# Gated cross-attention and a routed feed-forward: the causal mask and the row maxima put into one tile by GpSimd

## The chip, the cores and the metric

One core of one Trainium2 chip. The engines are TensorE (PE, with its weight loads PEld), VectorE (DVE), ScalarE (ACT), GpSimd (POOL) and SyncE (SP), whose queue issues most DMAs. The metric is the device time of one execution in microseconds, as the median of several executions.

## The reference

Only what matters is shown. There are 32 sequences of 128 tokens with 256 features, 16 heads of 16, 8 experts of 1024, and each token goes to its 2 best experts.

```python
q, k, v = proj(layernorm(x), w_q, b_q), proj(ctx, w_k, b_k), proj(ctx, w_v, b_v)
scores = einsum('bhqd,bhkd->bhqk', q, k) / sqrt(16)
attn = softmax(where(j <= i, scores, -inf))          # causal: S = 128
x = x + tanh(g_xattn) * (einsum('bhqk,bhkd->bhqd', attn, v) @ w_o.T + b_o)
xf = layernorm(x)
logits = xf @ Wr + br                                 # 8 experts
weights = softmax(where(logits >= second_best, logits, -inf))
h = gelu(einsum('td,edh->eth', xf, W1) + b1)
x = x + tanh(g_ffn) * einsum('etd,te->td', einsum('eth,ehd->etd', h, W2) + b2, weights)
```

## The kernel before, in words

The program has two halves. The first (`attention_and_routing`) does the attention of all 32 sequences, finds each token's experts and scatters the token rows to regions of experts in HBM (`xs_dram`). The second (`experts`) goes through 39 tiles of 256 rows, applies two layers, and adds the results to the output rows by indirect DMA. The change lies in the first half.

**Groups and slots.** The first half takes 16 groups of 2 sequences (`GT = 2`, blocks b = 0 and 1). One pass of `it(g, ...)` of each engine has 8 slots (`QUADS`), n = 0 to 7. A slot deals with one quad, that is 4 heads of one block: 128x512 scores. Passes are pipelined: in the pass of group g the quads of g are done, the projections of g + 1 are made, the output projection, second normalisation and logits of g - 1, and the routing table and scatters of g - 2. The order on each engine is the order in which the slots are written down; engines meet at counting semaphores only.

**A quad's way.** In slot n PE writes the scores of quad n with the queries on partitions into PSUM bank `SB[n % 2]` (L899; the constant rows of `qfull` and `kfull` make later keys very negative, so that the maximum is over the keys seen). DVE takes the maxima over keys (L746, `rowmax`, 128x4 in 16 bits). In slot n + 1 PE makes the transposed scores less their maximum in bank `TB` ("ST" below) in three steps, all accumulated in one bank: the causal mask by a product of `ident16` with `maskT`, 512 columns wide (L955); the negative maxima by four products of `rowmax`, broadcast, with `negident` (L958); the scores by four products of 96 rows (L962). ACT takes the exponential (L583, `probs`). In slot n + 3 PE multiplies by the values, with a column of ones for the sums (L979, "PV" below). After four quads of a block DVE divides (`normalise`, L695 and L696, result `ao`), in slot 7 for block 0 of group g and in slot 3 for block 1 of group g - 1.

**What else stands in the slots, as far as it is spoken of below.**
- PE: transposes of `cin` and the product with `wo` (slot 0), the key product and transposes of `xn` (1), values (2), the query product (3), the product with `wo` of block 1 (4), logits (7). The first product with `wo` waits for `logits_read` and `w_read`, which DVE gives in slot 7.
- ACT: `cT` after the exponential of slot 0, `keys` in slot 1, `queries` in slot 3, and parts of the expert weights' split in slots 1 to 6.
- DVE: slot 0 `xn` (L763), `x2` of block 0 (L706), then the scale of the expert weights (`ebits`, `wnow`, L771 to L778, with copies to `wscale` and `wsquares`); slot 1 `k_rest` (L675), the normalised rows `pay` of block 0 (L715, `norm2`), the routing table; slot 2 its end (`sel`, L808), third part of keys (L687); slot 3 `va`, `q_rest`; slot 4 `x2` of block 1 (L706) and its variance; slot 5 `pay` of block 1 (L715) and the third part of queries (L687); slots 2, 3, 6 and 7, behind the maxima, the low half of the weights (L756, both inputs in SBUF); slot 7 the statistics of the next input, the weights' sum `wsum` (L845), the logits `lg` (L848), the top two, and the masks `msk` (f32) and `msk16`.
- POOL: slots 1 and 5 the power -1/2 of a variance (L497), which `norm2` of the same slot waits for; slot 5 the input with the output bias added (`xb`, L504, 128x512 with two inputs); slots 4 to 7 one scatter each (L512); slot 7 the power for `xn` (L521).

DVE's wait for the buffer of `rowmax` is for the ST two quads before:

```python
dve.wait_ge(s_psum, g * QUADS + n + 1)
when(dve, n >= 2 or there(g - 1), st_psum, g * QUADS + n - 1)
dve.tensor_reduce(rowmax[n % 2][:, :], SB[n % 2][:, :]..., AX, ALU.max).then_inc(max_ready, 1)
```

Of the kernel before, what the change touches and what calls it, by code (L numbers as in the profile page):

```python
# [12 lines left out]
P = 128  # L13
# [18 lines left out]
MASKED = -1e30  # L32
# [62 lines left out]
def bass_flamingo(nc, x, ctx_in, g_xattn, g_ffn, w_q, b_q, w_k, b_k, w_v, b_v, w_o, b_o,  # L95
# [4 lines left out]
    with ExitStack() as stack:  # L100
        def sb(name, shape, dt=F32):
            return stack.enter_context(nc.sbuf_tensor(name, shape, dt))
# [25 lines left out]
        ident16 = sb("ident16", [P, P], BF16)  # L128
        qsteps, ksteps, maskT = (sb(name, [P, P], BF16) for name in ("qsteps", "ksteps", "maskT"))
# [44 lines left out]
def attention_and_routing(nc, env):  # L174
# [3 lines left out]
     xs_dram, w_dram, bank, qst, kst, qfull, kfull, ident, negident, ident16, qsteps, ksteps, maskT, earlier, ones16, rank1,  # L178
# [4 lines left out]
         "negident", "ident16", "qsteps", "ksteps", "maskT", "earlier", "ones16", "rank1", "rank0", "ones8", "region0",  # L183
         "base", "mostsel", "tgx", "tgf", "gates_in", "power", "wscale", "wsquares", "padrow",
         "b1t", "stage", "split", "all_slots", "wts", "tile_no_int", "numbers_made", "weights_in"))
    with ExitStack() as stack:
# [21 lines left out]
        rowmax = [sb(f"rowmax{i}", [P, 4], BF16) for i in range(2)]  # L208
        probs = [sb(f"probs{i}", [P, 4, P]) for i in range(4)]
# [14 lines left out]
        msk, msk16 = sb("msk", [P, GT, E]), sb("msk16", [P, GT, E], BF16)  # L224
# [31 lines left out]
        s_psum, max_ready = sem("s_psum"), sem("max_ready")  # L256
# [81 lines left out]
        with nc.Block() as block:  # L338
# [107 lines left out]
            def _(pool):  # L446
# [4 lines left out]
                step.later(pool.memset(maskT[:, :], 0.0))  # L451
# [40 lines left out]
                def it(g, par, half, stays, stayed):  # L492
                    for n in range(QUADS):
                        if n in (1, 5) and there(g - 1):
# [4 lines left out]
                        if n == 5 and there(g + 1):  # L499
# [53 lines left out]
            def _(act):  # L553
# [12 lines left out]
                def it(g, par, half, stays, stayed):  # L566
                    g1, p1 = g + 1, 1 - par
                    for n in range(QUADS):
# [8 lines left out]
                        q, pg = (QUADS - 1, g - 1) if n == 0 else (n - 1, g)  # L577
# [67 lines left out]
            def _(dve):  # L645
# [6 lines left out]
                dve.wait_ge(consts, 9)  # L652
# [4 lines left out]
                step.later(dve.tensor_scalar(negident[:, :], ident[:, :], -1.0, None, ALU.mult))  # L657
                dve.tensor_copy(ident16[:, :], ident[:, :]).then_inc(dve_consts, 1)
# [756 lines left out]
```

## Time and profile before

| | us |
|---|---|
| median of 3 runs | 938.75 (936.92 to 939.47) |
| the profiled execution | 942.84 |
| its span, first to last instruction | 940.9 |
| scores and maxima of the 16 groups (L746) | 34.8 to 444.9 |
| PE busy in the span | 846.5 |
| DVE busy | 600.4 |
| ACT busy | 442.3 |
| POOL busy | 257.6 |

In rows of the profile, PE is the matmuls and PEld the weight loads beside them. The number after the time is the length; what stands in square brackets is the engine's idle time before the instruction and what ended it. In the groups by line, "x128" is the count, and the number behind the busy time is the mean length in ns.

### The profile page before, as it was taken

Reading aid. Unit: us, or ns where it says so; the run is one execution under the profiler, and the core shown is the slowest. Engines: PE = TensorE matmul, PEld = TensorE weight load, DVE = VectorE, ACT = ScalarE, POOL = GpSimd, SP = SyncE. Lnnn points to the kernel's source line nnn. Section 1 sums busy time; section 2 is a strip of 40 time slices with the busy share of each in tenths; the row PEclk is TensorE's granted clock in tenths of the full one; section 3 lists DMA queues with packets and bytes.
Section 4 is the critical chain, followed back from the end, with each engine's and each line's share of the span. In section 5 each row is a group of like instructions: output and inputs, shape, how many; then the busy total and the mean of one; then the engine's idle time right before and its main releaser. Section 6 shows DMA issues by size and latency. Waiting matters only on the chain. (4 is left out here: it accounts for less than half of the span.)

```text
span 940.9 us, 24425 instructions
## 1 busy us (share of the span) xinstructions
PE 846.5 (90%) x7600; PEld 750.5 (80%) x7601; DVE 600.4 (64%) x1521; ACT 442.3 (47%) x962; POOL 257.6 (27%) x239
## 2 busy tenths in 40 slices
PE   3599999999999999999539999999999999999990
PEld 2488888888888888888338789998989998989980
DVE  2357888888888888887636555555555555555540
ACT  2155555655555555654224444554444455544440
POOL 3001333222332333323210322232332232223332
PEclk9699999999999999999659999999999999999996
DMA  8765666665667787864388432323233233322222
GB/s 185 141 135 132 158 152 129 139 155 156 155 159 202 188 185 176 174 164 156 130 288 295 87 53 48 54 53 53 48 50 52 48 59 50 51 48 36 30 24 25
DMA packets 87944, 108.77 MB, mean 116 GB/s; under 512 B 12832, under 2 KB 81568, under 8 KB 85664
## 3 DMA queue, kind: packets, MB, share of 16 engines
q1 hardware_dynamic: 72448, 87.17, 37.4%
q0 software_dynamic: 14304, 19.15, 12.7%
q8 instruction: 60, 0.98, 0.5%
q10 hardware_dynamic: 1088, 1.11, 0.4%
q14 instruction: 44, 0.36, 0.1%
HBM read 46.82 MB, written 34.36 MB: 86 GB/s over the span
## 5 line engine op out<-in xcount | busy, mean ns | idle before, releaser
L1220 POOL DMA_INDIRECT out_rows<-yg,xs x78 | 126.6, 1624 | 332.7 <-ACT yg L1262 190.3
L1352 PE MATMUL bank<-xh,wts 128*128 128x256 f16 x1872 | 214.2, 275 | 0.0
L1368 PE MATMUL bank<-wts,hh 128*128 x1872 | 210.6, 273 | 0.0
L1352 PEld LDWEIGHTS bank<-xh,wts 128*128 x1872 | 185.0, 99 | 22.5
L1368 PEld LDWEIGHTS bank<-wts,hh 128*128 128x128 f16 x1872 | 183.2, 98 | 21.2
L1252 ACT ACTIVATE hf<-bank,b1t,gscale 128x256 f32<-128x256 f32 x312 | 154.7, 562 | 24.3 <-PE bank L1352 24.3
L979 PE MATMUL bank<-va,probs 128*128 128x102 f32 x1024 | 139.7, 278 | 8.1 <-DVE ao L696 8.1
L979 PEld LDWEIGHTS bank<-va,probs 128*128 128x128 f32 x1024 | 124.2, 192 | 10.7 <-DVE ao L696 6.2
L1262 ACT ACTIVATE yg<-yb,xs 128x256 f32<-128x256 f32 x78 | 35.4, 500 | 199.5 <-DVE yb L1301 199.5
L583 ACT ACTIVATE probs<-bank 128x512 f32<-128x512 f32 x128 | 76.9, 601 | 101.8 <-PE bank L962 95.2
L1291 DVE SCALAR_TENSOR_TENSOR hh<-hf,hscale,hh 128x512 f16<-128x512 f32 x156 | 117.1, 751 | 5.6
L512 POOL DMA_INDIRECT token_rows<-pay,slots x64 | 76.2, 1190 | 130.4 <-DVE slots L811 93.0
L746 DVE TENSOR_REDUCE rowmax<-bank 128x4 bf16<-128x512 f32 x128 | 87.7, 686 | 22.8 <-PE bank L899 12.8
L1301 DVE SCALAR_TENSOR_TENSOR yb<-bank,yscale,b_all 128x512 f32<-128x512 f32 x39 | 29.2, 750 | 108.7 <-PE bank L1368 108.7
L1290 DVE TENSOR_SCALAR hh<-hf,hscale 128x512 f16<-128x512 f32 x156 | 76.1, 488 | 20.9 <-ACT hf L1252 12.3
L1275 DVE SCALAR_TENSOR_TENSOR xh<-bank,xh 128x512 f16<-128x512 f32 x39 | 27.0, 691 | 70.3 <-ACT xh L1243 70.3
L899 PE MATMUL bank<-wts 128*128 128x128 bf16 x512 | 49.9, 220 | 17.2 <-DMA wts<-queries 15.8
L497 POOL TENSOR_TENSOR rs<-mv,power 128x1 f32<-128x1 f32 x32 | 17.7, 552 | 153.3 <-DVE mv L665 153.3
L899 PEld LDWEIGHTS bank<-wts 128*128 128x128 bf16 x512 | 40.2, 102 | 20.5 <-issue 17.6
L955 PE MATMUL bank<-maskT,ident 128*128 128x512 bf16 x128 | 49.1, 383 | 6.4 <-issue 3.1
L958 PEld LDWEIGHTS bank<-negident,rowmax 128*128 128x128 bf16 x512 | 39.5, 98 | 19.1 <-issue 0.6
L962 PE MATMUL bank<-wts 96*128 96x128 bf16 x512 | 49.7, 219 | 0.0
(169 smaller groups left out, 1082.0 us busy)
## 6 DMA issues: line engine op xcount, KB each, us to landing
wts<-in_W SPq DMA_DIRECT2D x16, 1024.0 KB, 7.9
wts<-keys SPq DMA_DIRECT2D x96, 128.0 KB
wts<-queries SPq DMA_DIRECT2D x96, 128.0 KB
xs<-token_rows SPq DMA_DIRECT2D x39, 272.0 KB
split_weights<-wts SPq DMA_DIRECT2D x8, 1024.0 KB, 4.6
wts<-split_weights SPq DMA_DIRECT2D x8, 1024.0 KB
xin<-in_x SPq DMA_DIRECT2D x16, 256.0 KB, 4.0
cin<-in_ctx_in SPq DMA_DIRECT2D x16, 256.0 KB, 4.2
```

The costliest lines, as they stand in the source:

```text
L512: pool.indirect_dma_start(out=xs_dram[:, :], out_offset=bass.IndirectOffsetOnAxis(ap=slots[par][:, b, r:r + 1], axis=0), in_=pay[par][:, b ...
L583: act.activation(probs[q % 4][:, :, :].rearrange("p a q -> p (a q)"), TB[q % 2][:, :], ACT.Exp, scale=float(DK) ** -0.5).then_inc(exp_read ...
L746: dve.tensor_reduce(rowmax[n % 2][:, :], SB[n % 2][:, :].rearrange("p (a k) -> p a k", a=4), AX, ALU.max).then_inc(max_ready, 1)
L899: last = pe.matmul(ps[:, a * P:(a + 1) * P], qfull[par][:, h, tok], kfull[par][:, h, tok], start=True, stop=True)
L962: last = pe.matmul(ps[:, a * P:(a + 1) * P], kst[i][:, h, tok], qst[i][:, h, tok], start=False, stop=a == 3)
L979: last = pe.matmul(OB[:, h * VA:(h + WIDE) * VA], probs[m % 4][:, a, :], va[i][:, b, h, :].unsqueeze(1).to_broadcast([P, WIDE, VA]), start ...
L1220: pool.indirect_dma_start(out=out[:, :], out_offset=bass.IndirectOffsetOnAxis(ap=numbers, axis=0), in_=yg[m % 2][:, half, :], in_offset=No ...
L1252: last = act.activation(hf[:, c, :], HB[quarter][:, c % 2 * TILE:(c % 2 + 1) * TILE], ACT.Gelu, bias=b1t[:, bass.ds(e, 1), c], scale=gscal ...
L1290: step(dve.tensor_scalar(high, full, hscale[:, bass.ds(e, 1)], None, ALU.mult))
L1291: dve.scalar_tensor_tensor(out=hh[b][:, 1, c, :].rearrange("p c t -> p (c t)"), in0=full, scalar=hscale[:, bass.ds(e, 1)], in1=high, op0=A ...
L1352: last = pe.matmul(HB[c // 2][:, c % 2 * TILE:(c % 2 + 1) * TILE], wts[:, bass.ds(expert[1], 1), at:at + P], xh[b][:, xp, k, :], start=q = ...
L1368: last = pe.matmul(YB[b][:, half * D:(half + 1) * D], hh[b][:, hp, c, half * P:(half + 1) * P], wts[:, bass.ds(expert[0], 1), at:at + D], ...
```

## The change

GpSimd makes a tile `cover` (128x512, 16 bits, two buffers in the memory of `first_xs[0]`, which is not otherwise used before the second half). An `affine_select` reads `rowmax`, broadcast over 128 columns, and puts +1e30 where the key lies after the query. PE's ST becomes, for each head, a product of `cover` with `negident` and the scores' product; the product with `maskT` and the tiles `maskT` and `ident16` go. ST and the exponential lag the maxima by two slots in place of one; PV stays at three. DVE's maxima wait for `cover_ready` and not for ST, and the cover waits for the maxima and for the ST two quads before. Besides:
- `xb` moves from slot 5 to slot 6, the scatters from slots 4 to 7 to slots 3, 4, 5 and 7. In slots 1 and 5 the cover stands ahead of the power.
- The f32 `msk` goes, and the routing reads `msk16`.
- DVE no longer copies `wnow` to `wscale` for each weight; four small operations in `tile_table` make the scales from `wsquares`, and the copy to `wsquares` is no longer waited for at once.
- One GpSimd memset, one `affine_select` and one DVE copy go from the constants.

```diff
-MASKED = -1e30
+MASKED = 1e30
...
+        cover = [env["first_xs"][0][:, :, :].rearrange("p h r -> p (h r)")[:, 256 * i:256 * i + 256].bitcast(BF16)
+                 .rearrange("p (a k) -> p a k", a=4) for i in range(2)]
...
-                pool.affine_select(out=maskT[:, :], in_=maskT[:, :], compare_op=ALU.is_ge,
-                                   fill=MASKED, base=0, pattern=[[1, P]],
-                                   channel_multiplier=-1).then_inc(consts, 1)
...
                     for n in range(QUADS):
+                        if there(g):
+
+                            pool.wait_ge(max_ready, g * QUADS + n + 1)
+                            settled(pool)
+                            when(pool, n >= 2 or there(g - 1), st_psum, g * QUADS + n - 1)
+                            settled(pool)
+                            pool.affine_select(out=cover[n % 2][:, :, :],
+                                               in_=rowmax[n % 2][:, :].unsqueeze(2).to_broadcast([P, 4, P]),
+                                               compare_op=ALU.is_ge, fill=MASKED, base=0, pattern=[[0, 4], [-1, P]],
+                                               channel_multiplier=1).then_inc(cover_ready, 1)
                         if n in (1, 5) and there(g - 1):
...
-                        if n == 5 and there(g + 1):
+                        if n == 6 and there(g + 1):
...
-                        if n >= 4 and there(g - 2):
-                            b, r = (n - 4) // 2, n % 2
-                            if n == 4:
+                        if n in (3, 4, 5, 7) and there(g - 2):
+                            b, r = divmod((3, 4, 5, 7).index(n), 2)
+                            if n == 3:
...
-                        q, pg = (QUADS - 1, g - 1) if n == 0 else (n - 1, g)
+                        q, pg = (QUADS + n - 2, g - 1) if n < 2 else (n - 2, g)
...
-                            when(dve, n >= 2 or there(g - 1), st_psum, g * QUADS + n - 1)
+                            when(dve, n >= 2 or there(g - 1), cover_ready, g * QUADS + n - 1)
...
-                            dve.wait_ge(w_scaled, g)
                             e = half - (1 - par)
-                            dve.tensor_copy(wscale[:, p1, bass.ds(e, 1)], wnow[:, p1:p1 + 1])
-                            step(dve.tensor_copy(wsquares[:, p1, bass.ds(e, 1)], wsum[:, p1:p1 + 1]))
+                            step.later(dve.tensor_copy(wsquares[:, p1, bass.ds(e, 1)], wsum[:, p1:p1 + 1]))
...
-                            step.later(dve.tensor_tensor(msk[:, :, :], lg[:, :, :],
-                                                         mx[:, :, 1:2].to_broadcast([P, GT, E]), ALU.is_ge))
...
-                        if there(g if n >= 1 else g - 1):
-
-                            tg, m, i = (g, n - 1, par) if n >= 1 else (g - 1, QUADS - 1, p1)
+                        if there(g if n >= 2 else g - 1):
+
+                            tg, m, i = (g, n - 2, par) if n >= 2 else (g - 1, QUADS + n - 2, p1)
                             tok = slice((m // 4) * P, (m // 4) * P + P)
-                            pe.wait_ge(max_ready, tg * QUADS + m + 1)
+                            pe.wait_ge(cover_ready, tg * QUADS + m + 1)
                             when(pe, m >= 2 or there(tg - 1), exp_ready, tg * QUADS + m - 1)
                             ps = TB[m % 2]
-                            pe.matmul(ps[:, :], ident16[:, :], maskT[:, :].unsqueeze(1).to_broadcast([P, 4, P]),
-                                      start=True, stop=False)
-                            for a in range(4):
-                                pe.matmul(ps[:, a * P:(a + 1) * P], rowmax[m % 2][:, a:a + 1].to_broadcast([P, P]),
-                                          negident[:, :], start=False, stop=False)
                             for a in range(4):
                                 h = 4 * (m % 4) + a
+                                pe.matmul(ps[:, a * P:(a + 1) * P], cover[m % 2][:, a, :],
+                                          negident[:, :], start=True, stop=False)
                                 last = pe.matmul(ps[:, a * P:(a + 1) * P], kst[i][:, h, tok],
-                                                 qst[i][:, h, tok], start=False, stop=a == 3)
+                                                 qst[i][:, h, tok], start=False, stop=True)
...
+    for layer in range(2):
+        step(dve.tensor_scalar(smallint[:, 2, :], wsquares[:, layer, :].bitcast(I32), 24, None, ALU.logical_shift_right))
+        step(dve.tensor_scalar(wscale[:, layer, :].bitcast(I32), smallint[:, 2, :], -one, 204 * one, ALU.mult, ALU.add))
```

## Rows read from the trace of the kernel before

**Rows 1.** The page's busy time of each engine: us, share of span, instructions

```profile
PE 846.5 (90%) x7600; PEld 750.5 (80%) x7601; DVE 600.4 (64%) x1521; ACT 442.3 (47%) x962; POOL 257.6 (27%) x239
```

**Rows 2.** Busy time in one stretch: us, each engine's busy (x instructions), clock, DMA

```profile
200.00:250.00 50.00, 48.14 (x439) 42.41 (x438) 41.87 (x123) 26.86 (x63) 15.58 (x16) 1.00 0.63 152
```

**Rows 3.** The first and the last of 14 such rows of L706, DVE's timeline: start, us

```profile
76.27 0.48 DVE L706 SCALAR_TENSOR_TENSOR x<-bank,tgx,xb 128x256 f32<-128x256 f32 x1 [1.01 <-PE bank L880]
...
418.32 0.48 DVE L706 SCALAR_TENSOR_TENSOR x<-bank,tgx,xb 128x256 f32<-128x256 f32 x1 [1.01 <-PE bank L880]
```

**Rows 4.** DVE's timeline through one group: start, us, instruction, idle before it

```profile
196.61 0.87 DVE L675 SCALAR_TENSOR_TENSOR k_rest<-bank,bqk,keys 128x256 f32<-128x256 f32 x2 [0.60 <-ACT keys L562]
...
205.69 0.88 DVE L675 SCALAR_TENSOR_TENSOR q_rest<-bank,bqk,queries 128x256 f32<-128x256 f32 x2 [0.49 <-ACT queries L562]
...
208.09 0.48 DVE L706 SCALAR_TENSOR_TENSOR x<-bank,tgx,xb 128x256 f32<-128x256 f32 x1 [0.93 <-PE bank L880]
...
209.46 0.69 DVE L746 TENSOR_REDUCE rowmax<-bank 128x4 bf16<-128x512 f32 x1
...
210.13 1.36 DVE L715 TENSOR_SCALAR pay<-x,mv,rs 128x256 f32<-128x256 f32 x1
...
211.42 0.68 DVE L687 TENSOR_TENSOR queries<-q_rest,queries 128x512 bf16<-128x512 f32 x1
...
212.62 0.73 DVE L756 SCALAR_TENSOR_TENSOR wts<-wts,wnow 128x512 f32 x1
...
213.56 0.42 DVE L696 TENSOR_TENSOR ao<-bank,rden 128x256 f32<-128x256 f32 x1
...
214.49 0.74 DVE L756 SCALAR_TENSOR_TENSOR wts<-wts,wnow 128x512 f32 x1
...
216.52 0.16 DVE L848 TENSOR_TENSOR lg<-bank,br_all 128x16 f32<-128x16 f32 x1
...
222.70 0.88 DVE L675 SCALAR_TENSOR_TENSOR k_rest<-bank,bqk,keys 128x256 f32<-128x256 f32 x2 [0.70 <-ACT keys L562]
...
223.49 0.40 DVE L715 TENSOR_SCALAR pay<-x,mv,rs 128x256 f32<-128x256 f32 x1
```

**Rows 5.** TensorE's timeline in the same group: start, us, instruction, idle before it

```profile
216.93 1.03 PE L880 MATMUL bank<-wo_sb,aoT 128*128 128x256 f32 x4
...
222.19 0.38 PE L955 MATMUL bank<-maskT,ident 128*128 128x512 bf16 x1
...
222.41 0.38 PE L958 MATMUL bank<-negident,rowmax 128*128 128x128 bf16 x4
...
222.63 0.39 PE L962 MATMUL bank<-wts 96*128 96x128 bf16 x4
```

**Rows 6.** GpSimd's timeline in the same group

```profile
209.54 0.56 POOL L497 TENSOR_TENSOR rs<-mv,power 128x1 f32<-128x1 f32 x1 [5.78 <-DVE mv L665]
...
210.08 1.26 POOL L504 TENSOR_TENSOR xb<-xin,bo_all 128x512 f32<-128x512 f32 x1
...
211.52 1.49 POOL L512 DMA_INDIRECT token_rows<-pay,slots  x1 [0.18 <-issue]
...
213.31 0.97 POOL L512 DMA_INDIRECT token_rows<-pay,slots  x1 [0.30 <-issue]
```

**Rows 7.** The timeline at the start of the kernel

```profile
22.54 1.26 POOL L504 TENSOR_TENSOR xb<-xin,bo_all 128x512 f32<-128x512 f32 x1 [14.35 <-DVE bo_all L729]
...
22.82 1.52 DVE L687 TENSOR_TENSOR queries<-q_rest,queries 128x512 bf16<-128x512 f32 x1 [0.43 <-ACT queries L601]
```

**Rows 8.** The groups by line that price what is removed or added: busy, mean

```profile
L460 POOL TENSOR_SCALAR_AFFINE_SELECT ident<-ident 128x128 f32<-128x128 f32 x1 | 0.3, 299 | 0.0
...
L469 POOL IOTA ints<- 128x8 int32 x1 | 0.1, 139 | 0.0
```

**Rows 9.** The timeline where the two halves meet

```profile
474.64 0.17 DVE L1100 TENSOR_TENSOR yscale<-small 128x8 f32<-128x8 f32 x1
...
480.29 0.40 SPq L441 DMA_DIRECT2D xs<-token_rows  x1
```

More of the change, by code:

```diff
@@ L127, in bass_flamingo @@
         negident = sb("negident", [P, P], BF16)
-        ident16 = sb("ident16", [P, P], BF16)
-        qsteps, ksteps, maskT = (sb(name, [P, P], BF16) for name in ("qsteps", "ksteps", "maskT"))
+        qsteps, ksteps = (sb(name, [P, P], BF16) for name in ("qsteps", "ksteps"))
         earlier = sb("earlier", [P, P], BF16)
@@ L177, in attention_and_routing @@
     (x, ctx_in, g_xattn, g_ffn, w_q, b_q, w_k, b_k, w_v, b_v, w_o, b_o, W1, b1, W2, Wr, br, out,
-     xs_dram, w_dram, bank, qst, kst, qfull, kfull, ident, negident, ident16, qsteps, ksteps, maskT, earlier, ones16, rank1,
+     xs_dram, w_dram, bank, qst, kst, qfull, kfull, ident, negident, qsteps, ksteps, earlier, ones16, rank1,
      rank0, ones8, region0, base, mostsel, tgx, tgf, gates_in, power, wscale, wsquares, padrow,
@@ L223, in attention_and_routing @@
         lg, mx, lgs = sb("lg", [P, GT, E]), sb("mx", [P, GT, 8]), sb("lgs", [P, GT, E])
-        msk, msk16 = sb("msk", [P, GT, E]), sb("msk16", [P, GT, E], BF16)
+        msk16 = sb("msk16", [P, GT, E], BF16)
         ex, em, esum, erec = sb("ex", [P, GT, E]), sb("em", [P, GT, E]), sb("esum", [P, GT]), sb("erec", [P, GT])
@@ L255, in attention_and_routing @@
         v_psum, va_ready = sem("v_psum"), sem("va_ready")
-        s_psum, max_ready = sem("s_psum"), sem("max_ready")
+        s_psum, max_ready, cover_ready = sem("s_psum"), sem("max_ready"), sem("cover_ready")
         st_psum, exp_ready = sem("st_psum"), sem("exp_ready")
@@ L450, in _ @@
                 step.later(pool.memset(ksteps[:, :], -FUTURE / STEP))
-                step.later(pool.memset(maskT[:, :], 0.0))
                 step.later(pool.memset(earlier[:, :], 1.0))
@@ L651, in _ @@
                 step.later(dve.memset(ones16[:, :], 1.0))
-                dve.wait_ge(consts, 9)
+                dve.wait_ge(consts, 8)
                 step.later(dve.tensor_copy(rank0[:, :], ints[:, 0, :]))
@@ L656, in _ @@
                 step.later(dve.tensor_copy(base[:, :], ints[:, 2, :]))
-                step.later(dve.tensor_scalar(negident[:, :], ident[:, :], -1.0, None, ALU.mult))
-                dve.tensor_copy(ident16[:, :], ident[:, :]).then_inc(dve_consts, 1)
+                dve.tensor_scalar(negident[:, :], ident[:, :], -1.0, None, ALU.mult).then_inc(dve_consts, 1)
                 step.wait()
@@ L785, in it @@
                             dve.wait_ge(ex_ready, g - 1)
-                            step(dve.tensor_tensor(em[:, :, :], ex[:, :, :], msk[:, :, :], ALU.mult))
+                            step(dve.tensor_tensor(em[:, :, :], ex[:, :, :], msk16[:, :, :], ALU.mult))
                             for b in range(GT):
-                                step.later(dve.tensor_tensor_scan(cnt[:, b, :], ones8[:, :], msk[:, b, :], 0.0,
+                                step.later(dve.tensor_tensor_scan(cnt[:, b, :], ones8[:, :], msk16[:, b, :], 0.0,
                                                                   ALU.mult, ALU.add))
@@ L791, in it @@
                             step.later(dve.reciprocal(erec[:, :], esum[:, :]))
-                            step.later(dve.tensor_tensor(cm[:, :, :], cnt[:, :, :], msk[:, :, :], ALU.mult))
+                            step.later(dve.tensor_tensor(cm[:, :, :], cnt[:, :, :], msk16[:, :, :], ALU.mult))
                             step(dve.tensor_tensor(mostsel[:, :], mostsel[:, :], cnt[:, :, E - 1], ALU.max))
```

2 lines of the change are left out of this document (1 added, 1 removed).

## The prediction

> **What bounds the kernel now.** I read the page's busy times first, then the first half's busy time by stretches, then the timelines of DVE, PE and POOL through one group, and last who waited for whom. The page makes PE look like the bound, at 90% [rows 1]; in the stretch from 200 to 250 us, all of it first half, PE is busy 96% and DVE 84% of the time, at full granted clock [rows 2]. But the profile draws each matmul longer than the distance to the next, so a short gap of PE's does not show. The timelines show more: the pace is set by a loop that passes from one engine to the other. A group repeats every (418.32 - 76.27) / 13 = 26.31 us [rows 3]. I cut it at three places [rows 4].
> 1. From L706 (`x2`, second block) at 208.09 to the end of `ao` at 213.98: 5.89 us, all DVE without a pause. L706 itself had waited 0.93 us for PE.
> 2. From `ao` to `k_rest` (L675) at 222.70: 8.72 us. `ao` releases PE; PE's product with `wo` at 216.93 [rows 5] also needs `wsum` and `lg` (end 216.68), so DVE's slot 7 and PE's slot 7 end together, with 0.15 us over semaphore time of 0.10 to spare. Then ST, exp, `cT`, the key product and `keys` follow, and DVE waits 0.70 us.
> 3. From `k_rest` to the next L706, 196.61 to 208.09: 11.48 us, limited by PE; DVE waited 0.49 us at `q_rest` and 0.93 us at L706, so its own work is 10.06 us.
>
> **What is removed.** The mask product costs PE the distance from its start to L958's, 222.41 - 222.19 = 0.22 us [rows 5], times 128 = 28 us at most; it counts only in segments that PE limits. Segment 2 contains one ST (-0.22), segment 3 four (11.48 - 0.88 = 10.60). In segment 1 none counts. On DVE, the f32 `msk` and the copy of `wscale` with its waits go, about 0.4 us a group, after `lg` and before `k_rest`; DVE waits at `k_rest` anyway, so neither is worth anything. The two constants less at the start and the second PE lag at the end I cost at nothing: the first hides behind the loads, and the last PV keeps its slot. The four small DVE operations added at the table's end, each about 0.2 us like L1100 with its wait, end near 475.7 us, well ahead of the first load of `xs` at 480.29 [rows 9]; without that cover they would cost 0.8 us once.
>
> **What a cover costs.** No row shows a mask of 128x512. Half of the two-input sum of that size (L504, 1.26 us [rows 6]) is 0.63 us; a line through the 8 columns of L469 (139 ns) and the 128 of L460 (299 ns) gives 0.81 us at 512; four times L460 gives 1.20 us [rows 8]. I take 0.75 us, between the first two, since an instruction has a fixed part that four separate ones would pay four times, and keep 0.63 and 1.20. Eight of them add 6 us to POOL's 15.6 us in 50 [rows 2]: its throughput suffices; what matters is what stands behind each.
>
> **The powers queue behind the cover.** In slots 1 and 5 POOL now makes cover(n) before L497. Before, L497 at 209.54 ran while DVE did the maxima of slot 5, so that L715 followed at 210.13 [rows 4, 6]. Now cover(5) can start only after those maxima (210.15), and L715 needs: 0.10 for the semaphore, 0.75 cover, 0.56 power, 0.10 semaphore, so it starts at 211.66. Its 1.36 us shrinks to 0.41, the length of an undisturbed one (0.40 at 223.49), because the bias sum no longer runs beside it. The old start of the next, L687, was 211.42; the new is 211.66 + 0.33 = 211.99. Segment 1: +0.57. In slot 1, cover(1) must also wait for the ST of that slot, whose last product ends at 222.63 + 0.39 = 223.02 [rows 5], so at 222.80 without the mask product; 0.10 + 0.75 + 0.56 + 0.10 puts L715 at 224.35 in place of 223.49: +0.86 in DVE's part of segment 3.
>
> **The bias sum meets another instruction.** L715 beside L504 took 1.36 us for 0.40 [rows 4, 6], and L687, begun 0.28 us into an L504, 1.52 us for 0.68 [rows 4, 7]: DVE's instructions with both inputs in SBUF, and its `tensor_scalar` from SBUF to SBUF, stand still while POOL works on SBUF. The reverse shows too: the L512 at 211.52, just behind the start of an L687, took 1.49 us for the 0.97 of the next [rows 6]. So moving L504 to slot 6 frees L715, but cover(6) waits for L756 of slot 6 (212.62 + 0.74 = 213.36, now 213.93), ends at 214.72, and L504 begins about 214.77; L756 of slot 7, which came at 214.49 and now wants 215.06, is 0.29 us into it and loses the 0.84 us that L687 lost. That is upstream of `lg`, where PE has 0.15 us to spare: +0.69. Segment 2: +0.69 - 0.22 = +0.47. The Trainium skill (SBUF — State Buffer, Who interferes with whom) says that a DVE instruction with two SBUF inputs and a GpSimd one that reads SBUF exclude each other for the whole instruction; the two pairs of rows agree, and by that rule each cover is such an instruction. The GPSIMD Engine Reference of the Trainium skill (3.1) gives 769 ns for 512 elements of a simple GpSimd loop, which would make each cover 0.02 us dearer than I take it.
>
> **The covers meet others.** A cover's semaphore arrives about 0.1 us after the maxima end, when DVE's L756 has already begun (slots 2, 3, 6, 7), so the cover waits, not DVE. Behind it stand `va`, `q_rest`, `normalise` and `bn_stats`, which read PSUM or one operand: nothing. Only in slot 2 does another such operation follow, L808, which may lose nothing, if it is let in ahead of the waiting cover, or some 0.6 us; no row decides; I take 0.30. Segment 3 by DVE: 10.06 + 0.86 + 0.30 = 11.22; by PE 10.60; so 11.22 - 11.48 = -0.26.
>
> **The other moves.** Scatters now stand in slots 3, 4, 5 and 7, each behind a cover. They wait for nothing new and nobody in the first half waits for them before two groups on; a cover behind one waits at most its 1.5 us, and with two slots between cover and ST, 3.3 us each on average (26.31 / 8), ST does not see it. The extra slot also lets PE pass the maxima of slots 5 and 6, but these waits end at `ao` anyway. SP's queue has no new wait.
>
> **The sum.** 0.57 + 0.47 - 0.26 = +0.78 us a group, times 13 = +10.1 us. The first and the last group, where PE gains about 0.2 us in some slots and POOL falls behind in others, I take at zero. The profiled execution took 942.84 us for a span of 940.9; it would become 952.9. It stands 4.1 us above the median of the runs, so against those the forecast is 938.75 + 10.1 = 949 us. Bounds: a cover of 0.63 and nothing at L808 give 0.78 - 0.24 - 0.30 = +0.24, or 942; a cover of 1.20 and 0.60 at L808 give 0.78 + 0.90 + 0.30 = +1.98, or 964. So 942 to 964 is the forecast's own range.
>
> **Rivals.**
> - *PE sets the pace* (faster). If DVE's waits on POOL fall into time that it has over, each group loses the eight mask products, 1.76 us, 13 x 1.76 = 23 us, with the ends up to 28: 913 to 916 us. For it: 96% busy [rows 2]. Against it: DVE's unbroken 5.89 us in segment 1. It decides if the cover and power of slot 5 together take no more than the 0.95 us that L715 lost before. Chance 0.17.
> - *No collisions, only the powers.* If L504 misses L756 and L808 loses nothing: 0.57 - 0.22 - 0.55 = -0.20 a group, -2.6 us, 936 us. Here 0.55 is 11.48 less DVE's 10.06 + 0.86 with a cover of 0.75. For it: a shift of L504 by 1 us is enough. Against: DVE and POOL both start from the same maxima, so their distance is fixed. With a cover of 0.63, 0.12 goes off twice: -0.44 a group, 933 us. Where the power of slot 1 finds DVE waiting besides, segment 3 falls to PE's 10.60 and the sum to -0.65, 930 us. Chance 0.25, of which 0.14 stay within 0.3%.
> - *POOL late in slot 7.* Cover(6), L504, cover(7), L512 and L521 now stand in a row before `xn` of slot 0. L504 ends at 216.03, then come L756 of slot 7 (0.74), the cover (0.75), the scatter with its 0.30 of issue (1.27) and L521, which is like L497 with two columns (0.7 by estimate): 219.5. New `lg` ends at 216.68 + 0.57 + 0.84 = 218.09, and `xn` comes behind it and the maxima of slot 0, not before 219.5 either. A dearer cover tips it, by up to 0.5 us a group: 13 x 0.5 = 6.5 more, 955 us. Chance 0.10.
> - *The product is not really saved*: if the interleaved cover and score products pay for the mask product, ST keeps its 0.66 us: the 0.22 of segment 2 comes back, +1.0 a group, 952 us. Against it: PE issues four of either in 0.22 us now (222.41 to 222.63 [rows 5]), a weight load with each. Chance 0.03.
>
> **Numbers.** The forecast has 0.45; a measurement of this kernel tells about 0.3% (2.8 us) from no change. Slower: 0.45 less 0.02 near 941, plus 0.10 and 0.03 for the two rivals above it = 0.56. Same: 0.14 and 0.02 = 0.16. Faster: 0.17 and 0.11 = 0.28. The range of 8 in 10 leaves out the fastest 0.17 and a little at the top: 926 to 963.
>
> **What would show it.** In the new trace: no L955; ST 0.44 us long; covers of 0.75 us, longer where L756 came first; L715 of slot 5 0.41 us long but 1.5 us after the maxima, released by L497; L756 of slot 7 near 1.6 us; the group's period 27.1 us. I am wrong if L504 and L756 of slot 7 do not overlap, or if DVE's idle time before L715 is short, or if PE still runs without gaps and the period falls below 26.

## The result and the profile after

The changed kernel takes 979.00 us (972.58 to 986.14, four runs) against 939.04 us (936.92 to 939.47) for the kernel before on the same chip: a ratio of 1.043 (1.036 to 1.051). The forecast was 949 us with a range of 926 to 963. The sign was right, and the loss is four times as large as forecast, 40 us for 10. The profiled execution took 972.58 us for a span of 970.8 us, so it stands 6.4 us below the median. Its granted clock has a mean of 0.945; the three longer executions, of 978.24, 979.76 and 986.14 us, have 0.937, 0.933 and 0.928.

The page of the changed kernel, its busy times and the granted clock by fortieths of the span:

```profile
PE 841.9 (87%) x7472; PEld 757.5 (78%) x7473; DVE 595.8 (61%) x1492; ACT 439.1 (45%) x962; POOL 346.3 (36%) x365
PEclk9799899899999999998857999999999999999996
```

PE does less work than before (128 instructions fewer) in a longer span. The clock line has slices of 8 at the fifth and the eighth place, and from the nineteenth on (437 us) it sinks further, as it did from the twentieth in the kernel before. In the kernel before, the clock stood at full from 60 to 456 us. Now it falls to half, 1.2 GHz, four times in groups 2 to 5 (from 110.4, 141.1 and 171.8 us for 6.8 us each, before them from 83.1 us for 3.4 us), and again from 448.3 us, ahead of the last scores. The expectations below call such a fall an episode.

DVE's timeline through one undisturbed group of the changed kernel, to be laid beside [rows 4]; L680 is `k_rest`, L720 `pay`, L811 `sel`, L701 `ao`, L711 `x2`, L692 the third part of queries, L761 the low half of the weights, L851 `lg`:

```profile
319.45 0.88 DVE L680 SCALAR_TENSOR_TENSOR k_rest<-bank,bqk,keys 128x256 f32<-128x256 f32 x2 [1.22 <-ACT keys L568]
...
320.99 0.41 DVE L720 TENSOR_SCALAR pay<-x,mv,rs 128x256 f32<-128x256 f32 x1 [0.66 <-POOL rs L503]
...
324.49 0.72 DVE L811 TENSOR_TENSOR sel<-sel,pos 128x128 f32<-128x128 f32 x1
...
326.94 0.42 DVE L701 TENSOR_TENSOR ao<-bank,rden 128x256 f32<-128x256 f32 x1
...
331.32 0.48 DVE L711 SCALAR_TENSOR_TENSOR x<-bank,tgx,xb 128x256 f32<-128x256 f32 x1 [0.71 <-PE bank L881]
...
332.68 0.69 DVE L751 TENSOR_REDUCE rowmax<-bank 128x4 bf16<-128x512 f32 x1
334.90 0.41 DVE L720 TENSOR_SCALAR pay<-x,mv,rs 128x256 f32<-128x256 f32 x1 [1.53 <-POOL rs L503]
335.23 0.68 DVE L692 TENSOR_TENSOR queries<-q_rest,queries 128x512 bf16<-128x512 f32 x1
...
337.38 0.42 DVE L701 TENSOR_TENSOR ao<-bank,rden 128x256 f32<-128x256 f32 x1
337.72 0.68 DVE L751 TENSOR_REDUCE rowmax<-bank 128x4 bf16<-128x512 f32 x1
338.32 1.14 DVE L761 SCALAR_TENSOR_TENSOR wts<-wts,wnow 128x512 f16<-128x512 f32 x1
...
346.65 0.88 DVE L680 SCALAR_TENSOR_TENSOR k_rest<-bank,bqk,keys 128x256 f32<-128x256 f32 x2 [1.01 <-ACT keys L568]
```

GpSimd's timeline in the same group (the cover is shown as `xs`, whose memory it uses):

```profile
320.31 0.54 POOL L503 TENSOR_TENSOR rs<-mv,power 128x1 f32<-128x1 f32 x1
324.24 0.83 POOL L496 TENSOR_SCALAR_AFFINE_SELECT xs<-rowmax 128x512 bf16<-128x512 bf16 x1 [3.39 <-DVE rowmax L751]
...
333.71 0.62 POOL L496 TENSOR_SCALAR_AFFINE_SELECT xs<-rowmax 128x512 bf16<-128x512 bf16 x1 [0.99 <-PE bank L960]
334.31 0.56 POOL L503 TENSOR_TENSOR rs<-mv,power 128x1 f32<-128x1 f32 x1
...
336.85 0.82 POOL L496 TENSOR_SCALAR_AFFINE_SELECT xs<-rowmax 128x512 bf16<-128x512 bf16 x1 [0.62 <-DVE rowmax L751]
337.65 1.26 POOL L510 TENSOR_TENSOR xb<-xin,bo_all 128x512 f32<-128x512 f32 x1
```

And PE's timeline, where it now waits three times:

```profile
327.42 1.14 PE L977 MATMUL bank<-va,probs 128*128 128x102 f32 x8 [0.97 <-DVE ao L701]
...
335.37 0.44 PE L875 MATMUL bank<-ident,pay 128*128 128x128 f32 x2 [0.87 <-DVE pay L720]
...
337.86 1.14 PE L977 MATMUL bank<-va,probs 128*128 128x102 f32 x8 [1.36 <-DVE ao L701]
```

The prediction's three segments, at full clock, come out of these rows as follows (before, forecast, after). Segment 1, L711 at 331.32 to the end of `ao` at 337.80: 5.89, 6.46, **6.48**. Segment 2, to `k_rest` at 346.65: 8.72, 9.19, **8.85**. Segment 3, 319.45 to 331.32: 11.48, 11.22, **11.87**. The period of this group is thus 27.20 us, where the three forecasts add up to 26.87. The forecast of 27.1 was for the mean of the groups; the eight periods at full clock, of groups 6 to 13, have a mean of 27.28.

In the groups whose clock fell, segment 2 is longer: 10.56 to 12.11 us in groups 2 to 5. PE's timeline of one of them, through the same two waits:

```profile
138.16 0.44 PE L875 MATMUL bank<-ident,pay 128*128 128x128 f32 x2 [0.87 <-DVE pay L720]
...
140.65 1.63 PE L977 MATMUL bank<-va,probs 128*128 128x102 f32 x8 [1.36 <-DVE ao L701]
...
145.72 1.91 PE L881 MATMUL bank<-wo_sb,aoT 128*128 128x256 f32 x4
```

The product with `wo` takes 1.91 us where [rows 5] has 1.03. Busy time by stretches shows the same; the columns are those of [rows 2], the clock behind the engines:

```profile
134.00:141.00 7.00, 4.77 (x58) 4.41 (x57) 5.21 (x12) 4.49 (x12) 5.02 (x7) 1.00 0.59 134
141.00:148.00 7.00, 7.00 (x37) 6.45 (x37) 4.58 (x17) 0.38 (x1) 3.47 (x4) 0.51 0.72 213
```

PE was busy 4.77 of 7 us ahead of the fall, and is then busy without a pause at half speed.

**Where the 30 us between the two profiles went.** The last maxima end 30.8 us later than before (they start at 475.64 in place of 444.85), and what follows takes 0.9 us less. From the starts of slot 0's maxima: the 12 periods from group 2 to group 14 have a mean of 28.25 us for 26.31, which is 23.2 us; the first two give back 0.95; the last period and the last group cost 3.3 and 5.4. Of the 23.2, some 13 us is the longer period at full clock (12 x 1.1, with the mean period of 27.42 us that experiment 5 has without falls), and some 10 us the clock.

### The profile page after: what moved, and what is told of

It reads as the page before. It is cut to its first block and busy times, and to the rows that moved or that the text cites. A ratio compares the mean times of both kernels' runs of the same rounds, so it can differ in the third digit from the quotient of the medians.

```text
span 970.8 us, 24729 instructions
## 1 busy us (share of the span) xinstructions
PE 841.9 (87%) x7472; PEld 757.5 (78%) x7473; DVE 595.8 (61%) x1492; ACT 439.1 (45%) x962; POOL 346.3 (36%) x365
## 5 line engine op out<-in xcount | busy, mean ns | idle before, releaser
L496 POOL TENSOR_SCALAR_AFFINE_SELECT xs<-rowmax 128x512 bf16<-128x512 bf16 x128 | 97.4, 762 | 240.4 <-DVE rowmax L751 140.4
L977 PE MATMUL bank<-va,probs 128*128 128x102 f32 x1024 | 143.5, 283 | 37.4 <-DVE ao L701 35.3
L977 PEld LDWEIGHTS bank<-va,probs 128*128 128x128 f32 x1024 | 127.5, 196 | 42.4 <-DVE ao L701 27.6
L958 PE MATMUL bank<-negident,xs 128*128 128x128 bf16 x512 | 75.0, 223 | 0.3 <-POOL xs L496 0.3
L518 POOL DMA_INDIRECT token_rows<-pay,slots x64 | 67.2, 1050 | 22.1 <-issue 11.6
L960 PE MATMUL bank<-wts 96*128 96x128 bf16 x512 | 75.0, 223 | 0.0
L900 PEld LDWEIGHTS bank<-wts 128*128 128x128 bf16 x512 | 41.6, 105 | 19.0 <-issue 16.1
L960 PEld LDWEIGHTS bank<-wts 96*128 96x128 bf16 x512 | 51.4, 100 | 4.8 <-issue 1.9
```

The lines of the kernel that those rows point to most:

```text
L496: pool.affine_select(out=cover[n % 2][:, :, :], in_=rowmax[n % 2][:, :].unsqueeze(2).to_broadcast([P, 4, P]), compare_op=ALU.is_ge, fill=M ...
L900: last = pe.matmul(ps[:, a * P:(a + 1) * P], qfull[par][:, h, tok], kfull[par][:, h, tok], start=True, stop=True)
L960: last = pe.matmul(ps[:, a * P:(a + 1) * P], kst[i][:, h, tok], qst[i][:, h, tok], start=False, stop=True)
L977: last = pe.matmul(OB[:, h * VA:(h + WIDE) * VA], probs[m % 4][:, a, :], va[i][:, b, h, :].unsqueeze(1).to_broadcast([P, WIDE, VA]), start ...
```

## The experiments

All times are medians; ratios are to the kernel before, with the 95% interval.

**1. The powers ahead of the cover** (`pow_first`, from the changed kernel).

```diff
                     for n in range(QUADS):
+                        if n in (1, 5) and there(g - 1):
+                            b = n // 4
+                            pool.wait_ge(var2_ready, (g - 1) * GT + b + 1)
+                            pool.tensor_tensor(rs2[:, b:b + 1], mv2[:, b, 1:2], power[:, 0:1],
+                                               ALU.pow).then_inc(rstd2_ready, 1)
                         if there(g):
...
-                        if n in (1, 5) and there(g - 1):
...
```

> The changed kernel with only this edit: in slots 1 and 5 GpSimd makes the power before the cover, not behind it. Theory A (GpSimd's queue order costs 1.0 us a group, and the idle time it makes on PE lets PE's clock fall): the stretch from L706 to ao falls from 6.49 us to 5.1 to 5.5, the group's period at full clock from 27.3 to 26.0 or less, the half-clock episodes of groups 2 to 5 get fewer, and the time is 935 to 955 us. Rival B (the clock falls because the mask product is gone, whatever the waits): the stretch shortens the same, but the episodes stay, and the time is 958 to 968 us.

950.31 us, 1.014 (1.007 to 1.020): one exchange of two blocks gives back 29 of the 40 us. Part of this is the clock, which fell less: its profile has 17 us at half clock between 60 and 430 us (falls from 160.8, 188.1, 369.0 and 423.6 us), where the changed kernel's has 24. Segment 1 falls to 4.94 us, below the 5.89 of before, since `pay` neither waits nor meets `xb`; segment 3 falls to 11.11. But `xb` now collides in full in slot 7. The timeline of this kernel, GpSimd, DVE and then PE:

```profile
211.92 0.65 POOL L501 TENSOR_SCALAR_AFFINE_SELECT xs<-rowmax 128x512 bf16<-128x512 bf16 x1
212.12 2.23 DVE L761 SCALAR_TENSOR_TENSOR wts<-wts,wnow 128x512 f32 x1
212.52 1.27 POOL L510 TENSOR_TENSOR xb<-xin,bo_all 128x512 f32<-128x512 f32 x1
...
215.89 1.10 PE L881 MATMUL bank<-wo_sb,aoT 128*128 128x256 f32 x4 [1.17 <-DVE lg L851]
```

DVE's 0.74 us instruction starts inside a cover and is held until `xb`, next in GpSimd's queue, is over too: 1.49 us lost at once, `lg` late, PE waiting 1.17 us. Segment 2 is 9.93 us. That is the collision the prediction feared for the changed kernel, in another one, and it costs more than the 0.84 us of the forecast.

**2. One more product ahead of each ST** (`filler`, from the changed kernel): 512 columns of constants into the bank that ST then overwrites.

```diff
                             ps = TB[m % 2]
+                            pe.matmul(ps[:, :], negident[:, :], earlier[:, :].unsqueeze(1).to_broadcast([P, 4, P]),
+                                      start=True, stop=True)
```

> The changed kernel plus a product of 512 columns ahead of each ST, whose result is overwritten at once: PE does more work than in the changed kernel, and the output is the same. Theory A (some 20 of the 40 us are PE's half-clock episodes, and these come from PE having less to do): the granted clock is back at 0.955 or more, no episode lies in groups 2 to 14, and the time is 950 to 962 us although work was added. Rival C (all of the loss is waits): the product adds up to 0.2 us in each of 5 STs on the path, and the time is 979 to 992 us.

984.01 us, 1.049 (1.043 to 1.055), as rival C had it and not as theory A. The clock still fell, from 110, 168, 195, 257 and 311 us. Work put where PE does not wait does not fill the waits (PE still waits 1.14 us for `ao` in slot 7); it adds to the path (segment 3 went to 12.3 us).

**3. The mask product taken out of the kernel before** (`no_mask`). Nothing takes its place, so this kernel leaves out the causal mask. As in the change, the products of the maxima and of the scores now alternate head by head.

```diff
-                            pe.matmul(ps[:, :], ident16[:, :], maskT[:, :].unsqueeze(1).to_broadcast([P, 4, P]),
-                                      start=True, stop=False)
...
+                                pe.matmul(ps[:, a * P:(a + 1) * P], rowmax[m % 2][:, a:a + 1].to_broadcast([P, P]),
+                                          negident[:, :], start=True, stop=False)
```

> The kernel before without the mask product, all else as before (the exponentials include the keys after the query). Theory A with its PE part: segments 2 and 3 lose 0.2 and 0.9 us, the period falls from 26.3 to 25.3, and the time is 922 to 928 us if the clock holds. Rival B (losing the product alone makes PE's clock fall): half-clock episodes appear in groups 2 to 14 and the time is 940 to 965 us.

928.83 us, 0.989 (0.983 to 0.995). The segments are 5.89, 8.52 and 10.68 us, the period 25.28 for 26.31: the product is worth 1.03 us a group, against 0.22 + 0.88 = 1.10 by the prediction's step. Segment 1 has none of it. With the rest of the kernel as it was, the product is thus worth 10 us, not the 23 of the first rival. And the clock stays at full from 59.4 to 421.2 us, so the product's absence alone did not make it fall.

**4. Covers that nobody reads, in the kernel before** (`dead_cover`): the changed kernel's GpSimd block ahead of the powers; ST as before. DVE's maxima wait for it besides.

```diff
                     for n in range(QUADS):
+                        if there(g):
+                            pool.wait_ge(max_ready, g * QUADS + n + 1)
...
+                            when(pool, n >= 2 or there(g - 1), st_psum, g * QUADS + n - 1)
...
+                            pool.affine_select(out=cover[n % 2][:, :, :], ...).then_inc(cover_ready, 1)
...
                             when(dve, n >= 2 or there(g - 1), st_psum, g * QUADS + n - 1)
+                            when(dve, n >= 2 or there(g - 1), cover_ready, g * QUADS + n - 1)
```

> The kernel before, where GpSimd also makes the covers ahead of the powers as in the changed kernel, but nobody reads them; PE's work and its lag of one slot are as before, xb stays in slot 5. Theory A: the stretch from L706 to ao grows by 0.5 to 1.3 us (powers behind the cover, and xb now meets L687 or L756), the period is 27.0 to 27.8, and the time is 950 to 960 us if PE's clock holds at 0.95 or more. Rival D (PE's idle time makes the clock fall even with the mask product kept): episodes appear, and the time is 965 to 985 us.

995.63 us, 1.058 (1.050 to 1.065), above the ranges of both theories. Segment 1 is 7.46 us, since `pay` waits for the power and still meets `xb` there (1.35 us long), and the clock falls seven times between 107 and 419 us, though PE has all its work of before. PE's timeline in this kernel:

```profile
224.44 0.44 PE L887 MATMUL bank<-ident,pay 128*128 128x128 f32 x2 [1.13 <-DVE pay L727]
```

So it is not the mask product's absence that lets the clock fall: falls come with the product in place, and in experiment 3 they stayed away without it. They go with the waits.

**5. Work only in the two waits** (`idle_filler`, from the changed kernel): four products of constants in slot 6 ahead of the wait for `pay`, five in slot 7 ahead of the wait for `ao`, each 512 columns.

```diff
+                            if n == 7:
+                                free_bt(pe, g, 5)
+                                for _ in range(5):
+                                    pe.matmul(BT[:, :], negident[:, :], earlier[:, :]..., start=True, stop=True)
                             if m % 4 == 0:
                                 when(pe, b == 1 or there(tg - 1), ao_ready, tg * GT + b)
...
-                            pe.wait_ge(xn2_ready, (g - 1) * GT + b + 1)
                             free_bt(pe, g, 2 if n == 2 else 4)
+                            if n == 6:
+                                for _ in range(4):
+                                    pe.matmul(BT[:, :], negident[:, :], earlier[:, :]..., start=True, stop=True)
+                            pe.wait_ge(xn2_ready, (g - 1) * GT + b + 1)
```

> The changed kernel plus nine products of 512 columns a group whose result nobody reads, put where PE stands idle: four ahead of its wait for pay in slot 6, five ahead of its wait for ao in slot 7. The output is the same. Theory E (PE's clock falls because of these idle stretches, of 1.1 and 1.4 us): no half-clock episode in groups 2 to 14, segments 6.5, 8.9 and 11.9 us, period 27.3, time 952 to 958 us. Rival F (the episodes do not come from PE's idle time): they stay, and the time is 975 to 990 us.

960.74 us (960.17 to 961.88), 1.022 (1.020 to 1.025): 18 us faster than the changed kernel (20 by the two ratios) by giving PE 144 useless products. Its PE timeline:

```profile
295.19 1.02 PE L997 MATMUL bank<-earlier,negident 128*128 128x512 bf16 x4
296.46 0.44 PE L875 MATMUL bank<-ident,pay 128*128 128x128 f32 x2 [0.24 <-DVE pay L720]
...
297.46 1.24 PE L973 MATMUL bank<-earlier,negident 128*128 128x512 bf16 x5
298.95 1.14 PE L982 MATMUL bank<-va,probs 128*128 128x102 f32 x8 [0.24 <-DVE ao L701]
```

The waits shrink from 0.87 and 1.36 us to 0.24 each, nothing on DVE's path changes (6.49, 8.84, 11.87, period 27.42), and the clock stays at full from 39.8 to 446 us. PE's third wait, for `ao` in slot 3, was not filled: it stays, with 0.67 to 1.58 us in the 13 groups from 2 to 14, and no fall came behind it. The spread of the runs falls from 13.6 us to 1.7. Busy time from 50 to 450 us, first of the kernel before, then of the changed one, then of this one, each from its own profile:

```profile
50.00:450.00 400.00, 381.85 (x3505) 338.17 (x3503) 326.33 (x999) 218.40 (x496) 111.60 (x114) 1.00 0.67 162
```

```profile
50.00:450.00 400.00, 350.26 (x3149) 319.61 (x3148) 302.93 (x906) 203.13 (x467) 184.34 (x224) 0.96 0.63 151
```

```profile
50.00:450.00 400.00, 375.26 (x3377) 326.81 (x3374) 310.25 (x940) 208.06 (x477) 189.09 (x229) 0.99 0.64 157
```

**6. The small edits alone** (`small_edits`, from the kernel before): `xb` in slot 6, scatters in slots 3, 4, 5 and 7, `msk16` only, no copy to `wscale`; powers, mask product and lag as before.

```diff
-                        if n == 5 and there(g + 1):
+                        if n == 6 and there(g + 1):
...
-                        if n >= 4 and there(g - 2):
-                            b, r = (n - 4) // 2, n % 2
+                        if n in (3, 4, 5, 7) and there(g - 2):
+                            b, r = divmod((3, 4, 5, 7).index(n), 2)
...
```

> The kernel before with the side edits alone: xb in slot 6, scatters in slots 3, 4, 5 and 7, msk16 only, fewer copies of scales; mask product and lag as before. Theory G: the collision only moves from L715 of slot 5 to an L756, so the period stays within 0.3 us of 26.3, and the time is 934 to 944 us. Rival H: xb in slot 6 finds DVE free of two-operand work, the stretch from L706 to ao falls to 4.95 us, and the time is 925 to 930 us.

948.95 us, 1.010 (1.007 to 1.013), slower, against my expectation. Segments 5.86, 8.72, 11.48 are those of before. The profile shows why nothing is won: `pay` is down to 0.41 us, and in its place the low half of the weights in slot 6 takes 1.66 us for 0.74. The collision has moved within segment 1. It now stands just ahead of `ao`, PE waits 0.93 us there in place of 0.44, and the clock fell twice, from 215.9 and 349.0 us. The profiled run is only 2.5 us above that of before; what makes the median 8 us worse was not seen in a trace. The granted clock of the three longer executions, 0.949 to 0.954 for the profiled one's 0.958, points to more such falls in them.

**7 to 10. Where `xb` can stand.** It was moved from the pass before into the pass of its own group (it is read only one pass later): to slot 3, with SP's input loads put behind the copies of keys so that the earlier release fits, from the kernel before (`xb_own`) and, with the powers first and the scatters in slots 3, 5, 6 and 7, from the changed one (`pow_xb_own`); and to slot 0, with SP's order unchanged, from either (`before_xb0`, `pow_xb0`).

```diff
-                        if n == 5 and there(g + 1):
-                            arrived(pool, x_loaded, g + 1, 1 - par)
-                            when(pool, there(g - 1), x2_ready, g * GT)
+                        if n == 0 and there(g):
+                            arrived(pool, x_loaded, g, par)
+                            when(pool, there(g - 2), x2_ready, (g - 1) * GT)
...
-                            pool.tensor_tensor(xb[1 - par][:, :, :], xin[1 - par][:, :, :],
+                            pool.tensor_tensor(xb[par][:, :, :], xin[par][:, :, :],
...
```

The edit shown is that of `before_xb0`.

> The kernel before with xb made in the group's own pass in slot 3, where DVE reads PSUM for 3 us (and SyncE's loads of the next inputs put behind the copies of the keys, since they wait for xb). Theory G: L715 takes 0.41 us in every slot, the stretch from L706 to ao falls from 5.89 to 4.94 us, the other segments stay, and the time is 925 to 929 us. Rival I: PE or the loads then limit, and the time is 934 to 942 us.

931.80 us, 0.991 (0.988 to 0.994), between the ranges of the two theories: segment 1 is 5.06 us. What `xb` cost before is thus some 0.83 us a group.

> The changed kernel with the powers ahead of the covers, xb made in the own pass in slot 3, and scatters in slots 3, 5, 6 and 7. By the three segments: 4.94, 8.5 to 8.9 (L756 of slot 7 no longer blocked by xb) and 11.1 us, a period of 24.5 to 24.9 us; if PE's idle stretches stay short enough for its clock, the time is 915 to 924 us. If half-clock episodes come, 930 to 950 us.

983.31 us, 1.045 (1.041 to 1.048), a miss. Segment 1 is 4.94 and segment 3 11.1 us as expected, but PE now waits for the copies of queries, ten times for 1.8 to 3.6 us. The likely reason is SP's queue, where the moved loads stand ahead of these copies: SP waits 14 times for `xb`, 41.6 us in all, and in `xb_own` it never does. Its PE timeline:

```profile
321.42 0.61 PE L906 MATMUL bank<-wts 128*128 128x128 bf16 x4 [1.78 <-DMA wts<-queries]
```

The clock falls in every group and segment 2 is 11.7 to 14.7 us.

> The kernel before with xb made in the own pass in slot 0, behind the power for xn, where DVE has no large instruction with two SBUF operands. Expected from the segments: 4.94, 8.7 to 9.0 and 11.5 us, a period of 25.4, and 927 to 932 us. If xb there delays the power of slot 1 or the loads, segment 3 grows and the time is 934 to 942 us.

928.68 us, 0.989 (0.983 to 0.995), period 25.53.

> The changed kernel with the powers ahead of the covers and xb in the own pass in slot 0, behind cover(0); the scatters as in the change. Expected from the segments: 4.94, 8.5 to 8.9 and 11.1 us, a period of 24.6 to 24.9; if the clock holds 915 to 922 us, with half-clock episodes (PE still waits some 0.7 us for ao in slot 7) 925 to 945 us.

945.82 us, 1.005 (1.003 to 1.007). In a group at full clock the segments are 4.98, 8.70 and 11.12 us, which add up to 24.8, less than in any kernel so far. The mean period is 26.1 us: the clock fell six times for 3.4 us between 212 and 441 us.

**11 and 12. The last stalls.** First three products of constants ahead of the wait for `ao` in slot 7 (`pow_xb0_fill`), as in 5. Then besides that SP's load of expert weights, 1 MB a pass, put ahead of the next inputs' loads, where it stood behind them (`pow_xb0_w`).

```diff
                 def it(g, par, half, stays, stayed):
+                    if there(g):
+                        when(sp, there(g - 2), w_low, (g - 1) * 4)
...
+                        sp.dma_start(dst, src).then_inc(w_staged[par], 16)
                     if there(g + 2):
...
-                    if there(g):
-                        when(sp, there(g - 2), w_low, (g - 1) * 4)
...
-                        sp.dma_start(dst, src).then_inc(w_staged[par], 16)
```

> As the run pow_xb0, plus three products of 512 columns ahead of PE's wait for ao in slot 7, whose result nobody reads. If idle time there is what takes the clock, no episode lies in groups 2 to 14 and the time is 915 to 924 us, no more than pow_xb0; if not, it is as pow_xb0 or up to 3 us above it.

943.63 us over ten runs (935.23 to 953.24), 1.002 (0.999 to 1.005): no clear gain, and far from the 915 to 924 us expected. In the profiled execution, of 949.48 us, four falls remain, each behind a PE wait of 1.96 us or more, as this one of PE's timeline for a late transfer; one more wait, of 2.04 us, had no fall behind it:

```profile
110.35 0.40 PE L900 MATMUL bank<-wts 128*128 128x128 bf16 x4 [1.96 <-DMA wts<-queries]
```

> As the run pow_xb0_fill, with SyncE's load of the expert's weights (1 MB) put ahead of the next inputs' loads, so that it no longer waits for xb. In pow_xb0_fill PE stood idle 1.96 to 3.41 us before each episode in groups 2 to 14, behind late transfers (copies of queries, weights for ScalarE's split in slot 3, scatters). If the late weights are the cause, most episodes go, segment 1 stays at 4.95 to 5.5 us, and the time is 918 to 930 us. If the other transfers are, it stays at 938 to 950 us.

**926.69 us** (926.04 to 928.26), 0.986 (0.983 to 0.989): 1.4% below the kernel before, and the only one made from the changed kernel that is faster than it. Segments 4.95, 8.69 and 11.1 us, mean period 25.02, and full clock from 38.3 to 417.2 us.

## Why the prediction missed

**The step that failed is the one that is not there: the sum holds PE's clock at full.** The prediction read the full clock off [rows 2] and priced every wait of PE's at its own length. The waits it forecast itself, `pay` and `ao` later by some 0.6 us, cost twice: once on the path, and again where the clock falls behind them. Experiment 5 separates the two: 979.0 - 960.7 = 18 us is the clock, and 20 us stay (960.74 against 940.68 in the same comparison): 12 x 1.1 = 13 us of longer periods, and 7.6 us in the last period and the last group. Much the same two waits, 0.76 to 1.10 us for `pay` and 1.36 to 1.45 for `ao`, stand in every group of the changed kernel, and the clock fell in groups 2 to 5 of the profiled execution and not in 6 to 13. What picks the groups is not settled, nor which of the two waits it takes: they were filled together. The Trainium skill (TensorE: Matmul & The Clock Gate, A second HAM failure mode: psum-queue depth-cycling) says that short pauses between groups of matmuls, if frequent, make the clock fall and rise again. The trace and experiment 5 agree, and the prediction should have given this a chance of its own.

**The powers behind the cover (+0.57): right.** `pay` starts 1.53 us after the maxima end (333.37 to 334.90), forecast 1.51. Two errors cancel in it: the cover takes 0.62 us and not 0.75, but it starts 0.34 us after the maxima and not 0.10, as it had to wait for the ST of the same slot, which in slot 5 the prediction did not follow. Segment 1: +0.59.

**The bias sum meets the weights in slot 7 (+0.69 - 0.22 = +0.47): mechanism right, size too large.** L761 takes 1.14 us for 0.74, so it loses 0.40, not 0.84. The cover ahead of `xb` did not need 0.75 us from the end of slot 6's weights: it had been waiting, and ended 0.49 us after them, so `xb` was 0.67 us on when DVE arrived. Segment 2: +0.13. In experiment 1 DVE's instruction comes during the cover ahead of `xb`, and loses 1.49. Of the two pairs of rows that the prediction lays beside the rule of two SBUF inputs, only that of L687 has two such tensors; L715 reads one, with its scalars in columns.

**Segment 3 (-0.26): wrong, it is +0.39.** The two costs were sized well: 0.75 us more before `pay` in slot 1 for a forecast of 0.86 (its own terms, from 222.80, give 0.82), and 0.44 at L811 for 0.30 (0.72 us for 0.28, behind a cover that had been waiting since the maxima). DVE's own work with its wait for POOL, up to L711, came to 11.87 - 0.71 = 11.16 us, and 11.22 was forecast. What failed is the rule by which they were joined, the larger of DVE's total and PE's total. The segment is a chain through both. These are rows of DVE's timeline of the kernel before that [rows 4] leave out:

```profile
200.89 0.28 DVE L808 TENSOR_TENSOR sel<-sel,pos 128x128 f32<-128x128 f32 x1
...
202.92 0.42 DVE L696 TENSOR_TENSOR ao<-bank,rden 128x256 f32<-128x256 f32 x1
```

DVE's `ao` of block 1 now ends 7.91 us after `k_rest` starts (319.45 to 327.36; before 6.73, from 196.61 to 203.34), PE waits 0.97 us for it, and then needs 3.96 us of its own for PV, transposes and the product with `wo` until L711. 7.91 + 3.96 = 11.87. Before, PE had other work when `ao` came, did not wait for it, and L706 followed 4.75 us behind it. What PE saves in this segment ends in the new wait. In two of the groups the trace puts that wait down to ACT's `probs`, with 0.67 us.

**The edges, costed at nothing.** The last period and the last group cost 8.7 us. Three things are in it, and no run takes them apart. The clock now falls from 448.3 us, before the last scores, and not from 456.2 us, behind them. PE waits 3.85 us for `ao` ahead of the last maxima, where its longest such wait was 1.47 us. And DVE waits for the landing of a scatter, which the prediction had nobody wait for, and which shows nowhere in the kernel before; its timeline in the changed kernel:

```profile
431.42 0.41 DVE L720 TENSOR_SCALAR pay<-x,mv,rs 128x256 f32<-128x256 f32 x1 [1.79 <-DMA token_rows<-pay,slots]
```

In the last group of experiment 5 such a wait is 3.67 us and in that of experiment 12 it is 4.62, and these groups take 24.1 and 23.0 us for the changed kernel's 22.2 and 16.8 before. The first two groups gave back 0.95 as the prediction half expected.

**The rivals.** *PE sets the pace* is out: the product is worth 10 us in all (experiment 3), and PE waits longer than before, 0.87 and 1.36 us in segment 1 for 0.34 and 0.44. (Its 913 us should be 911: 938.75 - 28.) *No collisions* is out by L811 and L761. *POOL late in slot 7* is out: in the group shown GpSimd ended the power for `xn` at 341.87 us, and the maxima that DVE has ahead of `xn` ended at 342.63. *Not really saved* is out by experiment 3. None reached the time that came out: it lies 16 us above the range's top of 963, and the clock took 18.

**The small edits** were costed at nothing but for the move of `xb`. Experiment 6 has them, with that move, 1% slower than before, and 7 and 9 show that `xb` had a place worth -0.8 us a group.

## What to carry to other kernels

In an engine's in-order queue, put the short result that another engine waits for ahead of new long work: here that order was worth 29 of 40 us, with the falls of the clock that it spared. When a change makes a nearly full TensorE wait, price the waits twice, allow for a clock that falls behind them, and look at the granted clock group by group in the new trace; filling just those waits with idle products shows in one run how much is the clock. And join two engines' costs along the chain of who waits for whom, not as the larger of two totals.

## What was not expected of the hardware

- Pauses of 0.87 and 1.36 us, one soon after the other, in a PE otherwise nearly always busy came ahead of falls to 1.2 GHz; between group 2 and group 14 the falls of all kernels lasted 3.4, 6.8 or 10.2 us. One of 6.8 us cost up to 2.9 us of the group (segment 2 of 11.8 us for 8.84). Much the same pauses stood in groups 6 to 13 of the changed kernel, and no fall came behind them.
- With falls the spread of the runs is wider: 13.6 us in the changed kernel, where the granted clock was 0.928 to 0.945, and 1.7 us with its waits filled, where it was 0.957 to 0.960.
- A GpSimd instruction that has been waiting goes in ahead of DVE's next two-input instruction, even one right behind the other on DVE: L811 lost 0.44 us in this way, while GpSimd's mask of 128x512 alone takes 0.62 us. The Trainium skill (SBUF — State Buffer, Who interferes with whom) says that whichever issues first holds the shared port for the whole instruction; the rows agree, and experiment 1 adds that DVE's instruction, held by a cover, got no turn ahead of the `xb` queued behind it: 2.23 us for 0.74.
